# TensorE runs matmuls of no use during loads, at the head of each stage and in the first five items of each attention

## The chip, the cores and the metric

The kernel runs on one core of a Trainium2 chip. The core has five engines with a program each: TensorE (PE; its weight loads are listed as PEld), VectorE (DVE), ScalarE (ACT), GpSimd (POOL) and SyncE (SP, which issues DMAs). They meet through semaphores. The metric is the device time of one execution in microseconds (us). TensorE has two clock levels, 1.2 and 2.4 GHz; the profile shows the granted clock as a share of full speed.

## The reference

A residual stream x of 32 items of 128 rows by 128 columns passes through four layers of an attention-like block and a feed-forward-like block, each behind a layer norm:

```
x = x + _L0_xattn_ref(ctx, _layernorm(x), b, seq_len)      # 16 heads of 8, bias and length mask
x = x + _L0_ffn_ref(_layernorm(x), w1, w2)                 # summed experts
x = x + _L1_xattn_ref(_layernorm(x), ctx, lens, ...)       # depool
x = x + _L1_ffn_ref(_layernorm(x), mask, pos, router_w, ...)  # route 512 rows, attention, expand
x = x + _L2_xattn_ref(ctx, _layernorm(x), mask, b)         # 8 heads of 16
x = x + _L2_ffn_ref(_layernorm(x), w1, conv_w, conv_b, w2) # ternary weights, conv
x = x + _L3_xattn_ref(ctx, _layernorm(x), mask, ...)       # cross attention, 8 heads
x = x + _L3_ffn_ref(_layernorm(x), ...)                    # latent attention, 16 heads, causal; 4 experts
```

All of it is float32 in the reference, and the kernel returns the whole x.

## The kernel before, in words

Python code writes out the program of each engine, and each engine runs its program strictly in order; no scheduler moves anything. The work is cut into 15 stages, the list `phases`: prep (loads and constants), L0 attention, ffn0, depool, route, gather, L1 attention (four tiles, 16 heads), expand, L2 attention (8 heads), bit, cross, L3 attention (8 heads), latent, L4 attention (16 heads, causal), expert. At the end of each stage `phase_end` (L1022) drains an engine, raises `phase_done` and waits until all five have raised it. So no engine starts a stage before the slowest has ended the last one; what an engine waits for there is put down to L1022 in the profile.

Inside a stage, `steps` or `whole_steps` writes a software pipeline over the 32 items: in one step an engine works on several items at different lags. In an attention, PE's part is `attention_tensor`. At lag 1, `turns` transposes an item's queries and keys (L859, L860) and the split maxima of an item (L826). At lag 2, `halves` makes the raw scores: for each of four groups of heads it waits for a free PSUM bank (`raw_free`, which waits for `max_taken`, DVE's maximum over an earlier group), adds the bias (L746, `sel_bias`) and multiplies queries by keys (L753). DVE takes each row's maximum from that (L392, L397, L384). Later in the pipeline the scores are made again with the maximum taken off (L721 and L763, which multiplies by `sel_max`), ACT takes the exponential (L616, L620, L610), and PE multiplies by the values (L912). In L1 and L4 the first raw group comes with masks (`mask_strips`, `mask_whole`; the transposes of L799).

In ffn0, bit and cross the first PE work of an item is a transpose (L1041, L1033) of rows that ACT or DVE has normed; in route PE works twice for a short time (L1304, L1306); in latent PE first centres weights, then makes queries, then waits on `la_raw` and turns latents (L1799) into rows (L1806). `ident`, `identb` (bf16), `ones` and `sel_max` (bf16, 128 x 4 x 128) are constants that prep loads or makes.

PE had no work in prep. Before the change the only PE instructions are those that make results.

Of the kernel before, what the change touches and what calls it, by code (L numbers as in the profile page):

```python
# [135 lines left out]
def build(nc, t_in, out):  # L136
    with ExitStack() as ctx_:
# [26 lines left out]
        ones = sb("ones", [128, 128])  # L164
# [497 lines left out]
        def attention_tensor(pe, L, count, heads, mask_parts, mask, post_w):  # L662
# [34 lines left out]
            def halves(r_item, s_item, u):  # L697


                v = 1 - u  # L700
                whole = BANKS[L] == "items"
                r_groups = () if r_item is None else (u, 2 + u) if whole else (2 * u, 2 * u + 1)
                s_groups = () if s_item is None else (v, 2 + v) if whole else (2 * v, 2 * v + 1)
                if s_item is not None:
                    b, k = s_item
                    if u == (1 if whole else 0):
                        done(pe, "nmT_ready", b, count)
                    masked_scores = mask_parts and not cut_later
                    if whole and u == 0:
                        pe.wait_ge(*after("scores", b * 2 + 1))  # L710
                    for g in s_groups:
                        if whole and g == 0:
                            done(pe, "max_taken", b + 1, count)
                        elif not whole:
                            final_free(b, g)
                        bank, at = final_at(L, b, g, N)
                        for part in range(mask_parts if masked_scores else 0):
                            nc.tensor.matmul(ps[:, bank, at:at + N], mask(k, part), identb[:].unsqueeze(1).broadcast_to(four),
                                             start=part == 0, stop=False, skip_group_check=True)
                        if not masked_scores:  # L720
                            nc.tensor.matmul(ps[:, bank, at:at + N], kT[rows_of(g), k, :], qTm[rows_of(g), k, 0:N],  # L721
                                             start=True, stop=False, skip_group_check=True)
                    for g in s_groups if masked_scores else ():
                        bank, at = final_at(L, b, g, N)
                        nc.tensor.matmul(ps[:, bank, at:at + N], kT[rows_of(g), k, :], qTm[rows_of(g), k, 0:N],
                                         start=False, stop=False, skip_group_check=True)
                if r_item is not None:
                    b, k = r_item
                    if u == 0:
                        done(pe, "q_masked", b, count)  # L730
                        done(pe, "kT_ready", b, count)
                        if L in BIASES:
                            if b < 2:
                                pe.wait_ge(*after("early_nmT", b + 1))
                            else:
                                done(pe, "nmT_ready", b - 2, count)
                        if whole and b >= 4:
                            pe.wait_ge(*after("probs_ready", b - 3))
                    elif whole:
                        pe.wait_ge(*after("raw_scores", b * 2 + 1))  # L740
                    for g in () if whole else r_groups:
                        raw_free(b, g)
                    if L in BIASES:
                        for g in r_groups:
                            bank, at = raw_at(L, b, g, N)
                            nc.tensor.matmul(ps[:, bank, at:at + N], sel_bias[rows_of(g), :],  # L746
                                             nmT[rows_of(g), (k + 2) % RING, :].unsqueeze(1).broadcast_to([32, per, 128]),
                                             start=True, stop=False, skip_group_check=True)
                    for i in range(per):
                        for g in r_groups:  # L750
                            bank, at = raw_at(L, b, g, N)
                            dst = ps[:, bank, at + 128 * i:at + 128 * i + 128]
                            last = nc.tensor.matmul(dst, qTm[rows_of(g), k, 128 * i:128 * i + 128], kT[rows_of(g), k, :],  # L753
                                                    start=False, stop=True, skip_group_check=True)
                            if i == per - 1 and (raw_jobs(L) == 4 or g == r_groups[1]):
                                last.then_inc(sem("raw_scores"), 1)
                if s_item is not None:
                    b, k = s_item
                    for i in range(per):
                        for g in s_groups:  # L760
                            bank, at = final_at(L, b, g, N)
                            dst = ps[:, bank, at + 128 * i:at + 128 * i + 128]
                            last = nc.tensor.matmul(dst, sel_max[rows_of(g), i, :], nmT[rows_of(g), k, :], start=False,  # L763
                                                    stop=True, skip_group_check=True)
                            if i == per - 1 and (final_jobs(L) == 4 or g == s_groups[1]):
                                last.then_inc(sem("scores"), 1)
# [9 lines left out]
            def mask_strips(b, k):  # L776

                for a in range(2):
                    raw_free(b, a)
                if cut_later:  # L780
                    mask_tiles(b, (0, 1))
                    return
# [7 lines left out]
            def mask_whole(b, k):  # L790

                for a in range(2):
                    raw_free(b, 2 + a)
                if cut_later:
                    mask_tiles(b, (2, 3))
                    return
                for a in range(2):
                    for part in range(mask_parts):
                        nc.tensor.matmul(ps[:, raw_bank(L, b, 2 + a), 0:N], identb[:], mask(k, part).unsqueeze(1).broadcast_to(four),  # L799
                                         start=part == 0, stop=False, skip_group_check=True)  # L800
# [117 lines left out]
            def step(items):  # L918
# [12 lines left out]
                    mask_strips(*items[1])  # L931
                if L == "L0" and min(items) >= 3:
                    sum_products(pe, min(items) - 3)
            whole_steps(pe, count, TURN_LAG[post], step)


# [78 lines left out]

        phase_no = {}

        def phase_end(engine):

            n = phase_no.get(engine, 0) + 1  # L1020
# [68 lines left out]
            steps(act, B, [(1, take_rows(act))])  # L1089

        def ffn0_tensor(pe):
            def multiply(b, k):
                pe.wait_ge(*after("rowT", b + 1))
                wait_reuse(pe, after("added"), b, RING)
# [94 lines left out]
            steps(pool, B, [(3, take_patch)])  # L1189

        def depool_tensor(pe):
            def ends(b, k):
                pe.wait_ge(sem("dp_lens"), b + 1)
                wait_reuse(pe, after("dp_bound"), b, 2)
# [105 lines left out]
            nc.scalar.activation(small[:, 64:96], small[:, 0:32], ACT.Sin).then_inc(sem("ga_sines"), 1)  # L1300

        def route_tensor(pe):
            pe.wait_ge(sem("rt_wcol"), 1)
            nc.tensor.matmul(ps[0:B, 4, 0:128], wcol[:], ident[:], start=True, stop=True).then_inc(sem("rt_wT"), 1)  # L1304
            pe.wait_ge(sem("rt_coded"), 1)
            nc.tensor.matmul(ps[:, 5, 0:B], route_row[:, 384:512], ident[0:B, 0:B], start=True, stop=True)  # L1306
            nc.tensor.matmul(ps[:, 5, B:2 * B], route_row[:, 512:640], ident[0:B, 0:B], start=True,
# [6 lines left out]
        qD, kvD = q_all, kv_all  # L1314

        def gather_tensor(pe):
            pe.wait_ge(sem("ga_pick"), 1)


# [119 lines left out]
        pairT = probs[:, 1, 0:1024].rearrange("p (o t) -> p o t", o=2)  # L1439

        def expand_tensor(pe):


            for o in range(2):
                for T in range(TILES):
# [124 lines left out]
            steps(act, B, [(1, take_rows(act, dst=lambda k: xqT[:, k % 2, 1:129])), (2, silu)])  # L1570

        def bit_tensor(pe):
            def hidden(b, k):
                pe.wait_ge(*after("rowT", b + 1))
                wait_reuse(pe, after("bt_silu"), b, 2)
# [55 lines left out]
            steps(act, B, [(1, take_rows(act)), (2, take_kv), (3, take_q)])  # L1631

        def cross_tensor(pe):
            def queries(b, k):
                pe.wait_ge(*after("rowT", b + 1))
                wait_reuse(pe, after("cr_q"), b, 2)
# [141 lines left out]
            steps(act, PAIRS, [(0, scale), (1, take_turned), (3, take_v)])  # L1778

        def latent_tensor(pe):  # L1780
            pe.wait_ge(sem("la_weights"), 2)
            pe.wait_ge(sem("wo_loaded"), 16)
            nc.tensor.matmul(ps[:, 6, 384:384 + N_EXP3], wo_rows, w_h1[:, 320:], start=True, stop=True)
            nc.tensor.matmul(ps[:, 6, 0:320 + N_EXP3], centre[:], w_h1[:], start=True, stop=True).then_inc(sem("la_centred"), 1)

            def queries(b, k):
                pe.wait_ge(*after("rowT", b + 1))
# [4 lines left out]
                                 stop=True).then_inc(sem("used"), 1)  # L1792
            steps(pe, B, [(1, turn_x(pe)), (2, queries)])
            pe.wait_ge(sem("la_raw"), B)

            def turn_latents(p, k):
                pe.wait_ge(sem("la_latent"), 2 * p + 2)
# [280 lines left out]
                store(j)  # L2078

        def expert_tensor(pe):  # L2080
            def turn_block(j):
                pe.wait_ge(sem("bk_rows_%d" % (j % QUEUED)), 16 * (j // QUEUED + 1))
                if j >= 2:
# [294 lines left out]
        def row_counts(**more):  # L2378
# [2 lines left out]


        phases = [
            dict(sync=prep_sync, scalar=prep_scalar, gpsimd=prep_gpsimd, vector=prep_vector),
            dict(vector=lambda e: attention_vector(e, "L0", B, 16, True, False),
                 counts=attention_counts("L0", B, 16, False),
                 gpsimd=lambda e: attention_gpsimd(e, "L0", B, 16, True),
# [173 lines left out]
```

## Time and profile before

| | before |
|---|---|
| median of 3 runs | 1280.93 us |
| the three runs | 1286.64, 1275.42, 1280.93 us |
| profiled execution | 1290.61 us, its span 1288.9 us |
| mean granted TensorE clock in it | 0.894 |
| busy, share of the span | PE 86%, DVE 66%, PEld 63%, ACT 46%, POOL 28% |

The stages of the profiled execution begin at about these us of the span: prep 0, L0 17, ffn0 203, depool 226, route 290, gather 312, L1 334, expand 392, L2 420, bit 541, cross 684, L3 773, latent 900, L4 960, expert 1177. PE is the busiest engine in most of them; in depool it is DVE. The busy share is a mean over stages with different limits, so a stage is read by itself.

### The profile page before, as it was taken

What the parts mean: (1) busy time and instruction counts of PE and PEld (TensorE: products, weight loads), DVE (VectorE), ACT (ScalarE), POOL (GpSimd) and SP (SyncE); (2) the same over time, 40 slices, a digit from 0 to 9 for tenths busy, and PEclk for the clock granted to TensorE, in tenths of its full rate; (3) what the DMA queues carried; (4) which work ended last, traced back from release to release, by engine and by line L of the source; (5) the groups of instructions that cost most, each with busy time, mean ns of one, the idle gap of its engine ahead of it and who ended that gap; (6) DMA issues with size and microseconds to landing.
All of it is one profiled execution on the core that took longest, in us unless ns stands there. A gap on an engine that the chain in (4) does not pass through costs nothing. (4 is left out here: it accounts for less than half of the span.)

```text
span 1288.9 us, 36948 instructions
## 1 busy us (share of the span) xinstructions
PE 1110.1 (86%) x13741; PEld 811.3 (63%) x13741; DVE 845.1 (66%) x2666; ACT 591.9 (46%) x1413; POOL 357.2 (28%) x899
## 2 busy tenths in 40 slices
PE   2999998892894899689997999997899999896497
PEld 2888887672453677534444557885547887775497
DVE  4677766997636588679993226886845778953333
ACT  2688864565122466512222343554763445542243
POOL 1122220122040133400000001221433665573654
PEclk9999998795797599889996897998876999986899
DMA  9600000000000000110000005000000000024373
GB/s 288 186 8 3 4 3 2 2 2 1 1 2 1 2 3 3 65 68 1 1 1 0 1 1 194 3 3 2 1 1 2 3 4 3 11 74 117 129 235 109
DMA packets 36412, 49.43 MB, mean 38 GB/s; under 512 B 8365, under 2 KB 26161, under 8 KB 35904
## 3 DMA queue, kind: packets, MB, share of 16 engines
q1 hardware_dynamic: 32480, 40.55, 10.4%
q0 software_dynamic: 2752, 6.36, 1.4%
q8 instruction: 115, 1.88, 0.6%
q14 instruction: 57, 0.47, 0.1%
q10 hardware_dynamic: 1008, 0.16, 0.1%
HBM read 40.71 MB, written 11.81 MB: 41 GB/s over the span
## 5 line engine op out<-in xcount | busy, mean ns | idle before, releaser
L721 PE MATMUL ps<-qTm,kT 32*128 32x512 f32 (+1 forms) x1024 | 253.9, 560 | 3.7 <-ACT probs L620 3.4
L753 PE MATMUL ps<-kT,qTm 32*128 32x128 f32 x3200 | 254.9, 295 | 0.8 <-DVE kT L425 0.8
L753 PEld LDWEIGHTS ps<-kT,qTm 32*128 32x128 f32 x3200 | 230.5, 206 | 6.1 <-issue 3.4
L524 POOL CAST nm<-neg_max 128x16 bf16<-128x16 f32 (+1 forms) x132 | 26.9, 204 | 412.1 <-DVE neg_max L384 159.4
L620 ACT ACTIVATE probs<-ps 128x1024 f32<-128x1024 f32 x72 | 73.7, 1024 | 117.1 <-PE ps L763 116.6
L912 PE MATMUL ps<-probs,v_wide 128*32 128x128 f32 x3200 | 118.7, 283 | 9.1 <-DVE ctx_all L455 4.5
L397 DVE TENSOR_REDUCE neg_max<-ps 128x8 f32<-128x1024 f32 x72 | 87.9, 1221 | 57.3 <-PE ps L753 56.2
L721 PEld LDWEIGHTS ps<-qTm,kT 32*128 32x128 f32 x1024 | 86.2, 191 | 50.8 <-issue 39.8
L392 DVE TENSOR_REDUCE neg_max<-ps 128x4 f32<-128x512 f32 x128 | 82.2, 684 | 35.7 <-PE ps L753 35.6
L616 ACT ACTIVATE probs<-ps,bias_col 128x512 f32<-128x512 f32 x128 | 80.9, 683 | 37.5 <-PE ps L763 37.5
L411 DVE TENSOR_TENSOR qTm<-ps,hmask 128x512 f32<-128x512 f32 (+1 forms) x132 | 73.3, 555 | 37.4 <-ACT nmT L598 21.0
L912 PEld LDWEIGHTS ps<-probs,v_wide 128*32 128x32 f32 x3200 | 82.0, 112 | 24.9 <-issue 10.9
L763 PE MATMUL ps<-nmT,sel_max 32*128 32x128 bf16 x1600 | 97.2, 221 | 0.0
L1579 PE MATMUL ps<-tap_w,xqT 128*128 128x512 f32 x192 | 92.9, 621 | 0.0
L514 POOL COPY nm<-bias 128x12 bf16<-128x12 bf16 x96 | 19.0, 202 | 264.5 <-ACTq L1022 223.9
L626 ACT ACTIVATE pv<-ps 128x256 f32<-128x256 f32 x132 | 50.6, 383 | 77.1 <-PE ps L912 77.1
L610 ACT ACTIVATE probs<-ps,bias_col 128x1024 f32<-128x1024 f32 x64 | 71.3, 1114 | 32.0 <-PE ps L763 32.0
L879 PE MATMUL ps<-pv_pick,pv 128*128 128x72 f32 (+1 forms) x528 | 82.2, 279 | 0.9 <-ACT pv L626 0.9
L384 DVE TENSOR_REDUCE neg_max<-ps 128x8 f32<-128x1024 f32 x64 | 77.7, 1215 | 2.0 <-PE ps L753 1.7
L763 PEld LDWEIGHTS ps<-nmT,sel_max 32*128 32x128 bf16 x1600 | 72.5, 96 | 8.2 <-issue 5.9
L442 DVE RECIPROCAL inv_den<-ps 128x16 f32<-128x16 f32 (+1 forms) x132 | 30.2, 229 | 70.9 <-PE ps L879 67.3
L879 PEld LDWEIGHTS ps<-pv_pick,pv 128*128 128x128 f32 x528 | 70.5, 194 | 8.9 <-issue 1.8
(425 smaller groups left out, 2540.5 us busy)
## 6 DMA issues: line engine op xcount, KB each, us to landing
ctx_all<-in_W1T SPq DMA_DIRECT2D x38, 256.0 KB, 2.9
sorted_rows<-in_c_no_rows SPq DMA_DIRECT2D x1, 4940.0 KB, 20.8
kv_all<-sorted_rows SPq DMA_DIRECT2D x38, 130.0 KB, 2.6
ctx_all<-in_ctx SPq DMA_DIRECT2D x4, 1024.0 KB, 10.4
ctx_all<-in_ctxT SPq DMA_DIRECT2D x2, 2048.0 KB, 10.1
x_all<-in_x SPq DMA_DIRECT2D x4, 512.0 KB, 7.0
tap_w<-in_conv_wT SPq DMA_DIRECT2D x1, 768.0 KB, 6.6
out<-q_all,kv_all POOLq DMA_INDIRECT x38, 3.3
```

The costliest lines, as they stand in the source:

```text
L384: nc.vector.tensor_reduce(neg_max[:, k, 0:heads].rearrange("p (a h) -> p a h", a=2), ps[:, pair:pair + 2, 0:2 * N].rearrange("p a (h k) -> ...
L392: nc.vector.tensor_reduce(neg_max[:, k, per * g:per * g + per], ps[:, raw_bank(L, b, g), 0:N].rearrange("p (h k) -> p h k", h=per), AX.X, ...
L397: nc.vector.tensor_reduce(neg_max[:, k, H2 * u:H2 * u + H2].rearrange("p (a h) -> p a h", a=2), ps[:, 4 * u:4 * u + 2, 0:N].rearrange("p a ...
L411: nc.vector.tensor_tensor(qTm[:, k, 0:N].rearrange("p (i q) -> p i q", i=per), ps[:, 6, 0:128].unsqueeze(1).broadcast_to([128, per, 128]), ...
L616: nc.scalar.activation(probs[:, k % 2, N * g:N * (g + 1)], ps[:, final_bank(L, b, g), 0:N], ACT.Exp, bias=bias).then_inc(sem("probs_ready" ...
L620: nc.scalar.activation(probs[:, k % 2, 2 * N * u:2 * N * (u + 1)].rearrange("p (a n) -> p a n", a=2), ps[:, 2:4, 0:N], ACT.Exp, bias=bias) ...
L721: nc.tensor.matmul(ps[:, bank, at:at + N], kT[rows_of(g), k, :], qTm[rows_of(g), k, 0:N], start=True, stop=False, skip_group_check=True)
L753: last = nc.tensor.matmul(dst, qTm[rows_of(g), k, 128 * i:128 * i + 128], kT[rows_of(g), k, :], start=False, stop=True, skip_group_check=True)
L763: last = nc.tensor.matmul(dst, sel_max[rows_of(g), i, :], nmT[rows_of(g), k, :], start=False, stop=True, skip_group_check=True)
L879: last = nc.tensor.matmul(ps[:, 7, 256 + W * half:256 + W * half + W], pv[:, k % 2, 128 * half:128 * half + 128], pv_pick[:, 0 if heads == ...
L912: last = nc.tensor.matmul(ps[32 * j:32 * j + 32, 7, 128 * half:128 * half + 128], v_tile(k % 2, heads, 4 * half + j, i), probs[:, k % 2, 1 ...
L1579: last = nc.tensor.matmul(dst, xqT[:, k % 2, tap:tap + 128], tap_w[:, tap, :], start=False, stop=tap == 2)
```

## The change

`keep_busy(pe, spot, count)` writes `count` bf16 matmuls of 128 x 128 (`identb`) by up to 512 columns (`sel_max`) into a piece of PSUM, whose content nobody reads: the next real matmul there starts with `start=True`. `keep_busy_early` writes 44 float32 matmuls of 128 columns in prep, once `ones` is set. Heads: L0 16, ffn0 8, depool 14, route 64 and 11 more between its two PE groups, gather 9, L1 14, expand 8, L2 48, bit 46, cross 16, L3 8, latent 8 and then 12 and 20 inside, L4 8, expert 14; together 324 of 512 columns. In the first five items (`FILL`) of each attention, 4 x 512 columns per item are added right after the wait for the bank, ahead of the bias in L0, L2 and L3 (in L2 and L3 as pairs of 256 columns), and in `mask_strips` and `mask_whole` in L1 (all four items) and L4. Together these are 96 of 512 columns. No semaphore is new and no other engine's program changes; PE's later matmuls stay in their order. Behind the lines added, line numbers shift by up to 38 (L859 becomes L865, L746 becomes L748, L753 becomes L755).

PE at the head of L2, before: the last matmuls of expand (L1471), then the first item's transposes (L859, L860, L826), bias (L746) and raw scores (L753).

```order
L1471 MATMUL ps<-x_tiles,probs 128x128 x32
L859 MATMUL ps<-ident,row 128x128
L860 MATMUL ps<-ident,ctx_all 128x128
L826 MATMUL ps<-identb,nm 128x128
L746 MATMUL ps<-nmT,sel_bias 128x256 x2
L753 MATMUL ps<-kT,qTm 128x128 x4
```

PE at the head of L2 in the changed kernel (L1031 is the added matmul):

```order
L1500 MATMUL ps<-x_tiles,probs 128x128 x32
L1031 MATMUL ps<-sel_max,identb 128x512 x48
L865 MATMUL ps<-ident,row 128x128
L866 MATMUL ps<-ident,ctx_all 128x128
L832 MATMUL ps<-identb,nm 128x128
L1031 MATMUL ps<-sel_max,identb 128x256 x2
L748 MATMUL ps<-nmT,sel_bias 128x256
L1031 MATMUL ps<-sel_max,identb 128x256 x2
L748 MATMUL ps<-nmT,sel_bias 128x256
L755 MATMUL ps<-kT,qTm 128x128 x4
```

48 matmuls stand ahead of the first transpose, behind the stage's barrier, and two more ahead of each bias.

PE at the start of the program in the changed kernel, with what each row waits for: prep, then the head of L0 and its first items.

```order
L1038 MATMUL ps<-ones 128x128 [waits ones_set]
L1038 MATMUL ps<-ones 128x128 x43
L1031 MATMUL ps<-sel_max,identb 128x512 [waits phase_done]
L1031 MATMUL ps<-sel_max,identb 128x512 x15
L865 MATMUL ps<-ident,row 128x128 [waits q_row,ctx_loaded_0]
...
L1031 MATMUL ps<-sel_max,identb 128x512 [waits max_taken]
L748 MATMUL ps<-nmT,sel_bias 128x512
L1031 MATMUL ps<-sel_max,identb 128x512
L748 MATMUL ps<-nmT,sel_bias 128x512
L755 MATMUL ps<-kT,qTm 128x128 x8
```

The wait for the barrier now stands at the first matmul of the head, and the wait for DVE's maximum (`max_taken`) at the first added matmul of a group, no longer at the bias.

PE at the head of cross in the changed kernel, behind the last matmuls of bit (L1626):

```order
L1626 MATMUL ps<-w_q,qk_pad 128x128 x8
L1031 MATMUL ps<-sel_max,identb 128x512 x16
L1055 MATMUL ps<-ident,row 128x128
L1679 MATMUL ps<-bias_rows,onesb 128x256
L1681 MATMUL ps<-w_src,ctx_all 128x256 x2
```

16 stand ahead of the first item's transpose; the items themselves hold none.

```diff
--- before.py
+++ after.py
@@ -745,2 +745,4 @@
                             bank, at = raw_at(L, b, g, N)
+                            if b < FILL:
+                                keep_busy(pe, ps[:, bank, at:at + N], 512 // N)
                             nc.tensor.matmul(ps[:, bank, at:at + N], sel_bias[rows_of(g), :],
@@ -779,2 +781,4 @@
                     raw_free(b, a)
+                    if b < FILL:
+                        keep_busy(pe, ps[:, raw_bank(L, b, a), :])
                 if cut_later:
@@ -793,2 +797,4 @@
                     raw_free(b, 2 + a)
+                    if b < FILL:
+                        keep_busy(pe, ps[:, raw_bank(L, b, 2 + a), :])
                 if cut_later:
@@ -933,2 +939,3 @@
                     sum_products(pe, min(items) - 3)
+            keep_busy(pe, ps[:, 0, :], {"L0": 16, "L1": 14, "L2": 48, "L3": 8, "L4": 8}[L])
             whole_steps(pe, count, TURN_LAG[post], step)
@@ -1017,2 +1024,17 @@
 
+        FILL = 5
+
+        def keep_busy(pe, spot, count=1):
+
+            wide = spot.shape[1]
+            for _ in range(count):
+                nc.tensor.matmul(spot, identb[:], sel_max[:].rearrange("p i q -> p (i q)")[:, 0:wide], start=True, stop=True,
+                                 skip_group_check=True)
+
+        def keep_busy_early(pe):
+
+            pe.wait_ge(sem("ones_set"), 1)
+            for _ in range(44):
+                nc.tensor.matmul(ps[:, 0, 0:128], ones[:], ones[:], start=True, stop=True)
+
         def phase_end(engine):
@@ -1091,2 +1113,4 @@
         def ffn0_tensor(pe):
+            keep_busy(pe, ps[:, 7, :], 8)
+
             def multiply(b, k):
@@ -1191,2 +1215,4 @@
         def depool_tensor(pe):
+            keep_busy(pe, ps[:, 7, :], 14)
+
             def ends(b, k):
@@ -1302,4 +1328,6 @@
         def route_tensor(pe):
+            keep_busy(pe, ps[:, 7, :], 64)
             pe.wait_ge(sem("rt_wcol"), 1)
             nc.tensor.matmul(ps[0:B, 4, 0:128], wcol[:], ident[:], start=True, stop=True).then_inc(sem("rt_wT"), 1)
+            keep_busy(pe, ps[:, 7, :], 11)
             pe.wait_ge(sem("rt_coded"), 1)
@@ -1316,2 +1344,3 @@
         def gather_tensor(pe):
+            keep_busy(pe, ps[:, 7, :], 9)
             pe.wait_ge(sem("ga_pick"), 1)
@@ -1441,3 +1470,3 @@
         def expand_tensor(pe):
-
+            keep_busy(pe, ps[:, 7, :], 8)
 
@@ -1572,2 +1601,4 @@
         def bit_tensor(pe):
+            keep_busy(pe, ps[:, 7, :], 46)
+
             def hidden(b, k):
@@ -1633,2 +1664,4 @@
         def cross_tensor(pe):
+            keep_busy(pe, ps[:, 7, :], 16)
+
             def queries(b, k):
@@ -1780,2 +1813,3 @@
         def latent_tensor(pe):
+            keep_busy(pe, ps[:, 7, :], 8)
             pe.wait_ge(sem("la_weights"), 2)
@@ -1784,2 +1818,3 @@
             nc.tensor.matmul(ps[:, 6, 0:320 + N_EXP3], centre[:], w_h1[:], start=True, stop=True).then_inc(sem("la_centred"), 1)
+            keep_busy(pe, ps[:, 7, :], 12)
 
@@ -1794,2 +1829,3 @@
             pe.wait_ge(sem("la_raw"), B)
+            keep_busy(pe, ps[:, 7, :], 20)
 
@@ -2080,2 +2116,4 @@
         def expert_tensor(pe):
+            keep_busy(pe, ps[:, 7, :], 14)
+
             def turn_block(j):
@@ -2383,3 +2421,3 @@
         phases = [
-            dict(sync=prep_sync, scalar=prep_scalar, gpsimd=prep_gpsimd, vector=prep_vector),
+            dict(sync=prep_sync, scalar=prep_scalar, gpsimd=prep_gpsimd, vector=prep_vector, tensor=keep_busy_early),
             dict(vector=lambda e: attention_vector(e, "L0", B, 16, True, False),
```

## Rows read from the trace of the kernel before

**Rows 1.** Table by stretch: length, busy PE, PEld, DVE, ACT, POOL (us), clock, DMA, GB/s.

```profile
205.00:213.00 8.00, 6.83 (x30) 5.78 (x30) 4.38 (x17) 3.67 (x14) 0.78 (x2) 0.57 0.01 3
226.00:240.00 14.00, 9.14 (x35) 7.13 (x35) 11.52 (x65) 5.70 (x20) 1.19 (x3) 0.52 0.00 1
291.00:318.00 27.00, 5.68 (x126) 5.15 (x130) 19.91 (x112) 14.16 (x35) 6.87 (x21) 0.51 0.00 1
334.00:342.00 8.00, 8.00 (x50) 3.74 (x49) 4.25 (x11) 0.72 (x2) 0.00 (x0) 0.50 0.01 2
390.00:400.00 10.00, 6.25 (x17) 3.96 (x18) 4.58 (x20) 3.75 (x7) 1.34 (x3) 0.52 0.00 0
414.00:445.00 31.00, 20.49 (x194) 15.02 (x194) 18.03 (x55) 8.74 (x20) 3.31 (x18) 0.50 0.00 1
541.00:557.00 16.00, 4.77 (x7) 1.98 (x8) 11.80 (x30) 2.47 (x6) 7.07 (x8) 0.50 0.67 264
558.00:570.00 12.00, 11.83 (x47) 5.17 (x45) 9.73 (x41) 3.11 (x7) 0.00 (x0) 1.00 0.00 0
690.00:717.00 27.00, 27.00 (x61) 14.37 (x61) 3.61 (x13) 5.92 (x20) 0.00 (x0) 0.50 0.00 1
933.00:946.00 13.00, 11.98 (x31) 4.32 (x31) 3.75 (x6) 10.21 (x30) 3.56 (x5) 0.50 0.00 0
960.00:987.00 27.00, 25.54 (x265) 18.93 (x267) 13.56 (x18) 4.87 (x9) 4.99 (x11) 0.51 0.00 1
1177.00:1185.00 8.00, 5.48 (x22) 4.62 (x23) 1.97 (x12) 2.44 (x9) 0.00 (x0) 0.50 0.29 86
```

**Rows 2.** PE's timeline, L1: start, duration, operation, idle time before and its releaser.

```profile
339.52 2.77 PE L799 MATMUL ps<-kv_all,identb 128*128 128x512 bf16 x6
...
346.29 1.46 PE L799 MATMUL ps<-kv_all,identb 128*128 128x512 bf16 x6
```

**Rows 3.** PE's timeline, L0: turns of items and one raw group.

```profile
20.84 0.45 PE L859 MATMUL ps<-ident,row 128*128 128x128 f32 x1 [20.84 <-ACT row L584]
...
29.33 0.61 PE L746 MATMUL ps<-nmT,sel_bias 32*128 32x512 bf16 x2 [0.88 <-DVE neg_max L392]
...
55.97 0.27 PE L859 MATMUL ps<-ident,row 128*128 128x128 f32 x1
...
103.81 0.27 PE L859 MATMUL ps<-ident,row 128*128 128x128 f32 x1
```

**Rows 4.** PE's timeline, the opening of L1.

```profile
333.73 0.48 PE L859 MATMUL ps<-ident,kv_all 128*128 128x128 f32 x1 [3.60 <-SPq L1022]
```

**Rows 5.** ACT's (first row) and PE's timeline, L2.

```profile
419.57 0.20 ACT L259 ACTIVATE table_junk<-ones 128x1 f32<-128x1 f32 x1 [14.74 <-SPq L1022]
...
423.03 0.47 PE L859 MATMUL ps<-ident,row 128*128 128x128 f32 x1 [11.20 <-ACT row L584]
...
449.31 0.28 PE L859 MATMUL ps<-ident,row 128*128 128x128 f32 x1
...
487.24 0.28 PE L859 MATMUL ps<-ident,row 128*128 128x128 f32 x1
```

**Rows 6.** PE's timeline, the opening of bit.

```profile
553.08 0.60 PE L1577 MATMUL ps<-bias_rows,onesb 3*128 3x512 bf16 x1
```

**Rows 7.** ACT's (first row) and PE's timeline, cross.

```profile
683.81 0.20 ACT L259 ACTIVATE table_junk<-ones 128x1 f32<-128x1 f32 x1 [3.34 <-POOLq L1022]
...
686.87 0.44 PE L1033 MATMUL ps<-ident,row 128*128 128x128 f32 x1 [3.85 <-DVE row L269]
...
717.53 0.42 PE L1033 MATMUL ps<-ident,row 128*128 128x128 f32 x1
...
722.17 0.27 PE L1033 MATMUL ps<-ident,row 128*128 128x128 f32 x1
```

**Rows 8.** PE's timeline, the second half of latent.

```profile
933.89 1.05 PE L1799 MATMUL ps<-ident,o_sb 128*128 128x128 f32 x2 [5.39 <-ACT o_sb L1764]
```

**Rows 9.** PE's timeline, the opening of L4.

```profile
959.73 0.30 PE L859 MATMUL ps<-ident,q_all 128*128 128x128 f32 x1 [1.82 <-POOLq L1022]
```


## What I expect

> **What bounds the kernel now.** I read the views in this order: the table of the granted TensorE clock by stretch, PE's timeline at the heads of the stages, then what the other engines do there. The result gives a mean granted clock of 0.894 for the profiled execution. The table [rows 1] shows that this is no even shade: a stretch stands at 0.50 to 0.57 or at 1.00, which are TensorE's levels of 1.2 and 2.4 GHz. A mean of 0.894 then means (1 - 0.894) x 2 = 21% of the span, 273 us, at the lower level. Nearly all of it lies at heads of stages. The price shows at one line [rows 2]: six bf16 transposes of 128x512 take 2.77 us at the lower level and 1.46 at the higher, 0.46 and 0.24 each. A useless matmul has that size, so those are its two prices (0.45 and 0.23 below, as the six include one pipeline's end).
>
> What the lower level costs is not 273 us. Only PE's own time is halved, and only where PE sets the pace. In expand and L2 [rows 1] PE is busy 6.25 of 10 and 20.49 of 31 us; in the depool row DVE is busy 11.52 of 14, PE 9.14. In the cross row PE is busy 27.00 of 27 us at 0.50. That is the dearest stretch.
>
> Every stage ends in a barrier of five engines, and PE's program is in order. A head of useless matmuls therefore starts when the barrier opens, never in the idle time before it, and real work waits until it is through. So each head is weighed: what fits between the barrier and PE's first real operand is free, the rest is delay.
>
> **What a head costs.** In bit, dense work starts at 553.08 [rows 6], the row to 557 reads 0.50 and the row from 558 reads 1.00 [rows 1]: the clock rose after some 4.5 us. Two other rows are slower: in L1 PE is busy 8.00 of 8 us at 0.50, in cross 27.00 of 27. I take 4.5 us, thus ten matmuls at 0.45 and the rest at 0.23: 8 cost 3.6, 14 cost 5.4, 16 cost 5.9, 46 cost 12.8, 48 cost 13.2 us. Lower bound: all at 0.23; upper bound: all at 0.45. The useless matmuls inside the first items come when the clock should be up: 4 x 512 columns in each of five items, 20 x 0.23 = 4.6 us per attention (16 in L1: 3.7).
>
> **Stage by stage, gains positive, in us.** In brackets the bounds.
>
> - **Early 44 in prep**: beside loads; nothing of PE runs before 20.84 [rows 3]. 0.
> - **L0**: the turns L859 start 20.84, ... 55.97: six steps in 35.13 us, later 4.78 each (55.97 to 103.81 are ten) [rows 3]. At that pace six are 28.7: 6.4 lost. The page grants the first 50 us a clock of 1.00, but L859 takes 0.45 there and 0.27 at 55.97: durations decide, it is the lower level. In an early item PE waits 0.88 for DVE's maximum [rows 3], and a useless matmul sits behind that wait, in the loop, so some of the gain goes. The head of 16 ends about 0.3 to 2.5 late. +4.5 (0 to +6).
> - **ffn0**: PE 6.83 busy at 0.57 [rows 1], half of that at most; its 8 end by the first operand if the clock is still up from L0. +2 (0 to +3).
> - **Depool**: DVE covers it [rows 1]; were that cover gone, half of PE's 9.14. 0 (-1 to +2).
> - **Route and gather**: PE 5.68 busy in 27 us, mostly waiting for DVE; the 64, 11 and 9 lie in the waits. +2 (0 to +2.8).
> - **L1**: PE's wait of 3.60 before 333.73 is released by the barrier (L1022) [rows 4]: real work is ready, so 5.4 of delay, and 3.7 inside, against half of 8.00. -4.5 (-9 to 0).
> - **Expand**: 3.6 of delay against half of 6.25 plus a little. 0 (-2 to +1).
> - **L2**: the stage opens at 419.57 by ACT's first row, PE's first operand comes at 423.03 [rows 5]; the 11.20 idle there lies mostly before the barrier. 48 end at 432.8: 9.7 late. The seven steps to 449.31 take 26.3 where the later pace ((487.24 - 449.31)/12 = 3.16) gives 22.1; at most 4.2 come back, less the fills inside. -6 (-10 to -3).
> - **Bit**: 46 end near 554.2, real work began at 553.08 [rows 6]; up to half of its 4 cold us comes back. 0 (-2 to +2).
> - **Cross**: stage opens 683.81, first operand 686.87, eight steps in 30.66 us to 717.53; the next two take 4.64 [rows 7], so eight at the higher level are 18.6. 12.1 come back; 16 end 2.8 late. +9.5 (-4 to +12).
> - **L3**: no row quoted; built like L2, with 8: late by 1.8 to 3.6, back 2 to 3. -1 (-4 to +1).
> - **Latent**: the first 8 are about 1 late; the last 20 (4.6 to 9) lie in the 5.39 that PE waits for ACT's o_sb [rows 8]; PE is then busy 11.98 of 13 at 0.50, at most 6 back; ACT is busy 10.21 there and sets the next limit. +4.5 (-2 to +5).
> - **L4**: PE starts right at the barrier [rows 9]: 8 are 1.8 to 3.6 late; PE 25.54 busy of 27 at 0.51 [rows 1], 12.8 back, less most of 4.6 inside. +7 (0 to +10).
> - **Expert**: 14 ahead of ready work, 5.4, against half of 5.48 and a little behind it. -1.5 (-4 to +1).
>
> Sum: +16.5. On the profiled execution (1290.61 us, span 1288.9) that gives 1274.1; that run lies 9.7 above the median of the three shown. If the excess is a longer stay at the lower level in cross, whose 30 us are unlike any other stage, the change removes the excess too and 1274 holds; if it lies elsewhere, 1280.93 - 16.5 = 1264.4. I take **1268**, between the two.
>
> **Rivals.**
>
> *The heads run at the higher level from their start.* PE was at work shortly before most barriers, and at L4's opening L859 takes 0.30, nearly the 0.27 of the higher level [rows 3, 9]. Then ten matmuls cost 2.2 us less in each of L1, L2, bit, cross, L3, L4 and expert: 15 us less, about 1253 (1246 to 1260). Against it: 11.20 us idle before L2. Chance 0.24.
>
> *The lower level costs little, the useless work takes it back.* Where PE waits for DVE or ACT, a faster PE waits longer. With cross at 9.5, but 1 each for L0, ffn0 and gather, 2 for latent, 3 for L4, and -6, -8, -2, -3 for L1, L2, L3, expert, the sum is -1.5: about 1282 on the median, 1276 to 1293. For it: 20.49 of 31 in L2. Against it: 25.54 of 27 in L4. Chance 0.24. The Trainium skill, "TensorE: Matmul & The Clock Gate", Part 1 (The HAM clock gate), speaks for this one: it says "For modeling, the ramp penalty is <1% of a typical kernel span"; by that rule at most some 13 us could come back and the heads' delay would eat them. The trace disagrees with the premise, for 21% of this span is at the lower level, not one ramp.
>
> *Useless work does not lift the clock: slower.* In cross PE was busy for all of 27 us and the level stayed at 0.50. If the heads meet the same, each of the 420 (324 at heads, 96 inside items, counted in 512 columns) costs 0.45 and nothing comes back: L2 is 18 late, bit 9, L1 and expert 6 each, L0, L3, L4 and latent 4 to 13 each with what lies inside; 80 us in all if half the inside is hidden, 1300 for a third of the stages and 1370 for all. It decides from about 150 matmuls at 0.45 (150 x 0.22 = 33 us lost against the sum). Against it: the level did rise under bf16 transposes in L1 [rows 2] and under bit's matmuls. Chance 0.07.
>
> The forecast itself, 1260 to 1276, has 0.45.
>
> **Numbers.** About 1% tells this kernel from no change: below 1268 is faster, above 1294 slower. Faster: 0.23 of the second case and not quite half of the forecast, 0.43. Slower: 0.07, and 0.02 for the upper bounds of delay: 0.09. The rest, 0.48, is the same. The range 1250 to 1288 takes in the forecast, most of the heads-at-once case and most of the little-back case; some 0.07 lie below it, 0.12 above.
>
> **What would show it.** The granted clock should read 1.00 from about 5 us after each head; the mean should go from 0.894 to 0.95 or so. Cross: steps of 2.3 us from the first. L4: 0.27 for L859 from its first item. L2's first real matmul should come near 433, 13 us behind its barrier instead of 3.5; if it comes at 430, the heads ran at the higher level. L1 and L2 should each be longer than before by some 5 us. I am wrong if cross still has a long stretch at 0.50, if L1 and L2 don't lengthen, or if the gain comes from stages I put at 0.

## The result, and the profile after

The changed kernel takes 1309.91 us (median of 4 runs, 1307.55 to 1313.95) against 1278.18 us (4 runs): ratio 1.0245, 95% interval 1.0199 to 1.0291. It is slower by 2.5%; I had forecast 1268, with a range from 1250 to 1288. Its profiled execution took 1307.55 us, span 1305.7, with a mean granted clock of 0.946 where before had 0.894. So the change did what it says to the clock, and the time went the other way.

The page's lines for busy time and granted clock of the changed kernel:

```profile
PE 1184.8 (91%) x14262; PEld 831.9 (64%) x14289; DVE 845.5 (65%) x2666; ACT 590.4 (45%) x1413; POOL 357.2 (27%) x899
PEclk9599999899898799999999999999899999997899
```

One slice stands out: the second reads 5. It is L0. Cut at the barriers (the last drain of each stage), the stages last, in us. The columns "before, 3rd" and "before, 4th" are the third and fourth profiled executions of the kernel before, told below; at 1279.86 us the fourth is the one nearest the median.

| stage | before, 1st | before, 3rd | before, 4th | changed | heads only | no L0 items | items only | trimmed |
|---|---|---|---|---|---|---|---|---|
| L0 | 186.1 | 185.3 | 186.7 | 206.2 | 183.1 | 182.3 | 215.2 | 186.9 |
| L1 | 58.4 | 58.3 | 58.4 | 64.3 | 60.2 | 62.4 | 60.2 | 55.7 |
| L2 | 121.9 | 120.3 | 120.4 | 132.8 | 127.3 | 133.8 | 142.6 | 120.6 |
| bit | 142.4 | 143.4 | 143.4 | 140.9 | 140.8 | 141.3 | 142.7 | 140.9 |
| cross | 89.0 | 77.0 | 77.0 | 77.0 | 78.2 | 76.9 | 80.0 | 76.9 |
| L3 | 127.0 | 128.0 | 129.7 | 132.9 | 126.7 | 132.8 | 150.2 | 128.8 |
| latent | 59.9 | 55.9 | 59.6 | 56.4 | 56.8 | 56.4 | 59.7 | 56.7 |
| L4 | 217.5 | 210.5 | 214.4 | 210.4 | 213.9 | 213.0 | 214.2 | 210.8 |
| expert | 111.3 | 112.7 | 113.2 | 113.9 | 113.9 | 114.4 | 113.3 | 113.0 |
| the other six | 175.1 | 174.5 | 174.9 | 170.4 | 169.4 | 170.6 | 174.7 | 171.8 |
| all | 1288.3 | 1265.9 | 1277.6 | 1305.2 | 1270.3 | 1284.0 | 1352.6 | 1262.0 |

From the fourth execution of before to the changed kernel: L0 +19.5, L2 +12.4, L1 +6.0, L3 +3.3, expert +0.7; L4 -4.1, latent -3.2, bit -2.4, the other six -4.5; cross 0. That is the loss: four attentions lose 41 us, and all that was won elsewhere is 14. Of these 14, the 7.3 of L4 and latent are no wider than the spread of the kernel before: its third execution has 210.5 and 55.9 there, as short as the changed kernel, with no useless matmul in it.

**L0.** In what follows a filler is one of the useless matmuls, and a pair is two groups of heads with their two biases. The table by stretch of the changed kernel (columns as in [rows 1]):

```profile
22.00:32.00 10.00, 7.26 (x58) 4.44 (x59) 3.87 (x6) 2.62 (x10) 0.56 (x3) 0.98 1.04 291
32.00:42.00 10.00, 10.00 (x50) 5.39 (x49) 3.27 (x5) 1.31 (x5) 0.79 (x4) 0.50 0.84 230
42.00:52.00 10.00, 9.53 (x60) 5.44 (x60) 3.27 (x5) 3.55 (x9) 0.38 (x3) 0.50 0.70 185
52.00:62.00 10.00, 9.53 (x41) 4.10 (x42) 1.98 (x3) 2.24 (x7) 0.42 (x3) 0.50 0.64 180
```

The head did lift the clock, and it fell again at 31.6 us, with PE 9.5 to 10 of 10 us busy for the next 30. PE's timeline there, one raw group of an early item at the higher level, one at the lower, and the turns of two items (L865 was L859):

```profile
24.56 0.39 PE L1031 MATMUL ps<-sel_max,identb 128*128 128x512 bf16 x1 [1.44 <-DVE qTm L411]
24.88 0.39 PE L748 MATMUL ps<-nmT,sel_bias 32*128 32x512 bf16 x1
25.20 0.39 PE L1031 MATMUL ps<-sel_max,identb 128*128 128x512 bf16 x1
25.52 0.38 PE L748 MATMUL ps<-nmT,sel_bias 32*128 32x512 bf16 x1
...
43.54 0.47 PE L865 MATMUL ps<-ident,row 128*128 128x128 f32 x1
...
53.26 0.61 PE L1031 MATMUL ps<-sel_max,identb 128*128 128x512 bf16 x1
53.80 0.60 PE L748 MATMUL ps<-nmT,sel_bias 32*128 32x512 bf16 x1
54.33 0.61 PE L1031 MATMUL ps<-sel_max,identb 128*128 128x512 bf16 x1
54.87 0.60 PE L748 MATMUL ps<-nmT,sel_bias 32*128 32x512 bf16 x1
54.87 1.67 PE L755 MATMUL ps<-kT,qTm 32*128 32x128 f32 x11
...
57.11 0.47 PE L865 MATMUL ps<-ident,row 128*128 128x128 f32 x1
```

Each of the four now starts 0.32 us after the last at the higher level and 0.54 at the lower. Before, the two biases of 32 rows stood side by side as one row of x2 ([rows 3]), and the first raw product (L753) followed 0.37 us behind their start at 29.33:

```profile
29.70 1.94 PE L753 MATMUL ps<-kT,qTm 32*128 32x128 f32 x16
```

So up to its first raw product a pair costs 1.61 us (53.26 to 54.87) where two biases alone took 0.37, and one step from turn to turn takes 13.6 us (43.54 to 57.11), against 6.3 to 6.7 in the kernel before at the same level.

Two pairs per step explain 2.5 of the 6.9 us between 13.6 and 6.7. Most of the rest stands at L721, the scores with the maximum taken off, which belong to another item. In the kernel before, three of the eight of a step start among the raw products; here is PE's timeline of its step from 37.89 to 44.59:

```profile
38.62 1.43 PE L721 MATMUL ps<-qTm,kT 32*128 32x512 f32 x2
38.94 0.61 PE L746 MATMUL ps<-nmT,sel_bias 32*128 32x512 bf16 x2
...
39.63 1.06 PE L721 MATMUL ps<-qTm,kT 32*128 32x512 f32 x1
39.75 0.44 PE L753 MATMUL ps<-kT,qTm 32*128 32x128 f32 x2
...
41.03 2.32 PE L721 MATMUL ps<-qTm,kT 32*128 32x512 f32 x3
42.35 0.61 PE L746 MATMUL ps<-nmT,sel_bias 32*128 32x512 bf16 x2
```

In the changed kernel's step from 43.54 they stand in two blocks between the pairs:

```profile
44.26 2.28 PE L721 MATMUL ps<-qTm,kT 32*128 32x512 f32 x4
...
49.95 1.06 PE L721 MATMUL ps<-qTm,kT 32*128 32x512 f32 x1
...
50.80 2.52 PE L721 MATMUL ps<-qTm,kT 32*128 32x512 f32 x3
```

They hold PE nearly by themselves for 2.3 and 3.3 us (49.95 to the filler at 53.26), where it was 0.3 and 1.3 before (38.62 to 38.94, 41.03 to 42.35): some 4 us more. A filler of 128 rows parts not only the two biases of its pair but also the work of other items that ran beside it.

**L2's and cross's heads.** PE's timeline of the changed kernel:

```profile
441.32 11.96 PE L1031 MATMUL ps<-sel_max,identb 128*128 128x512 bf16 x47 [7.66 <-SPq L1044]
453.12 0.27 PE L865 MATMUL ps<-ident,row 128*128 128x128 f32 x1
```

```profile
715.00 4.75 PE L1031 MATMUL ps<-sel_max,identb 128*128 128x512 bf16 x15 [1.22 <-POOLq L1044]
719.59 0.27 PE L1055 MATMUL ps<-ident,row 128*128 128x128 f32 x1
...
723.19 0.27 PE L1055 MATMUL ps<-ident,row 128*128 128x128 f32 x1
725.41 0.27 PE L1055 MATMUL ps<-ident,row 128*128 128x128 f32 x1
```

L2's first real matmul now stands 12.3 us behind the barrier (440.86) where it stood 3.5 behind [rows 5]. Cross runs in steps of 2.2 us from the start; in [rows 7] its first eight took 3.8 each.

The seven fillers that the trace shows at the head of L3 took 1.67 us (from 791.83), and so did seven at the head of L4 (from 981.20): 0.24 each, the higher level from the start.

### The profile page after: what moved, and what is told of

It reads as the page before. It is cut to its first block and busy times, and to the rows that moved or that the text cites. A ratio compares the mean times of both kernels' runs of the same rounds, so it can differ in the third digit from the quotient of the medians.

```text
span 1305.7 us, 38009 instructions
## 1 busy us (share of the span) xinstructions
PE 1184.8 (91%) x14262; PEld 831.9 (64%) x14289; DVE 845.5 (65%) x2666; ACT 590.4 (45%) x1413; POOL 357.2 (27%) x899
## 5 line engine op out<-in xcount | busy, mean ns | idle before, releaser
L721 PE MATMUL ps<-qTm,kT 32*128 32x512 f32 (+1 forms) x1024 | 245.8, 543 | 3.6 <-ACT probs L620 3.1
L755 PE MATMUL ps<-kT,qTm 32*128 32x128 f32 x3200 | 241.6, 281 | 0.4 <-DVE kT L425 0.4
L755 PEld LDWEIGHTS ps<-kT,qTm 32*128 32x128 f32 x3200 | 214.0, 192 | 3.7 <-issue 2.4
L1031 PE MATMUL ps<-sel_max,identb 128*128 128x512 bf16 (+1 forms) x433 | 116.0, 402 | 39.6 <-SPq L1044 21.9
L721 PEld LDWEIGHTS ps<-qTm,kT 32*128 32x128 f32 x1024 | 83.8, 185 | 48.8 <-issue 38.0
L1031 PEld LDWEIGHTS ps<-sel_max,identb 128*128 128x128 bf16 x460 | 43.3, 106 | 104.4 <-issue 33.6
L765 PE MATMUL ps<-nmT,sel_max 32*128 32x128 bf16 x1600 | 94.3, 217 | 0.0
L514 POOL COPY nm<-bias 128x12 bf16<-128x12 bf16 x96 | 18.9, 201 | 250.3 <-ACTq L1044 210.5
```

What stands on the lines that cost most here:

```text
L1031: nc.tensor.matmul(spot, identb[:], sel_max[:].rearrange("p i q -> p (i q)")[:, 0:wide], start=True, stop=True, skip_group_check=True)
```

## The experiments

Ratios are to the kernel before, run beside it on the same chip, with their 95% intervals.

**1. Heads only.**

```diff
-        FILL = 5
+        FILL = 0
```

> The heads stay, the 96 matmuls inside the first items go (FILL = 0). Theory A, the matmuls inside cost the time: a 128-row matmul between matmuls of 32 rows stops those from running side by side, 1.7 us each in L0 at the lower level. Then L0 falls from 206 us to about 186, L3 from 133 to 128, L2 from 133 to 128, L1 from 64 to 61, and the time is about 1265 (ratio 0.99). Theory B, the clock fell in L0 at 31 us by itself and the matmuls inside cost only 0.23 to 0.45 each: L0 stays above 198, the time about 1295.

Measured: 1272.67 us, ratio 0.996 (0.9925 to 0.9995). L0 183.1, L2 127.3, L3 126.7, L1 60.2, as theory A said, if 8 us above its total. The 96 matmuls inside the items are worth 1.0245 - 0.996 = 2.9%, 36 us. The clock falls in L0 here too, to a shorter stretch (31 to 45 us):

```profile
31.00:45.00 14.00, 14.00 (x136) 11.37 (x136) 7.04 (x12) 6.43 (x17) 1.58 (x8) 0.51 0.73 198
```

So part of theory B holds: the fall comes without the items. What it costs depends on what then stands in the loop.

In L2 and L3 the items did hold the level, and the stages were longer all the same. Without them the clock falls soon behind the head, here in L2 and L3 of this run:

```profile
430.00:441.00 11.00, 10.19 (x113) 7.43 (x113) 5.76 (x10) 3.36 (x8) 2.33 (x13) 0.53 0.01 2
765.00:775.00 10.00, 9.79 (x91) 7.07 (x89) 5.03 (x10) 1.84 (x4) 2.08 (x11) 0.50 1.05 385
```

In the changed kernel it doesn't, in L2 and in cross and L3:

```profile
445.00:575.00 130.00, 123.24 (x1973) 87.60 (x1973) 82.37 (x195) 67.36 (x131) 38.76 (x159) 1.00 0.02 4
718.00:919.00 201.00, 196.53 (x2322) 135.75 (x2321) 106.79 (x308) 87.92 (x197) 24.64 (x128) 1.00 0.10 33
```

Yet L2 takes 132.8 us with the items and 127.3 without, L3 132.9 and 126.7.

**2. Items only.** The edit takes out all `keep_busy` lines of the heads and the early ones; those under `if b < FILL` stay.

> The 96 matmuls inside the first items stay, all heads and the early ones in prep go. Theory A: L0 pays 20 us or more, L1, L2 and L3 4 us each, L4 about the same as before, cross as long as before (77 to 89 us): about 1310 (ratio 1.025). Theory B: they cost 0.23 to 0.45 each, about 30 us at most, less what a higher clock returns: 1280 to 1290.

Measured: 1353.2 us, ratio 1.0612 (1.0542 to 1.0682), far beyond both. Without heads the useless matmuls meet the lower level and hold up the steps there. The table by stretch of this run, L2 and L3 (PE, then clock):

```profile
451.00:500.00 49.00, 45.15 (x311) 25.69 (x311) 14.68 (x32) 11.07 (x24) 4.86 (x24) 0.50 0.00 1
817.00:861.00 44.00, 43.03 (x290) 24.36 (x291) 12.35 (x25) 5.66 (x11) 3.61 (x19) 0.51 0.40 140
```

L2 and L3 stay at the lower level for 50 and 44 us; in the kernel before it was 25 and 14. PE is busy for 45.15 of 49 us and the level does not rise: matmuls of this mix did not lift it, and the slow stretch is longer with them. Cross, with nothing added, took 80.0 us here, the first hint that its 89 was not fixed.

**3. The change without the items of L0.**

```diff
-                            if b < FILL:
+                            if b < FILL and L != "L0":
```

> The change without the 20 matmuls inside L0's first five items; everything else as changed. Theory A: L0 returns from 206 to about 186 us and the time from 1310 to about 1290 (ratio to before 1.01). Theory B: the clock falls in L0 all the same, L0 stays above 198 and the time above 1300.

Measured: 1287.13 us, ratio 1.0079 (1.0041 to 1.0117); L0 182.3. The 20 useless matmuls in L0 alone cost 1309.91 - 1287.13 = 23 us, 1.1 each, where I had 0.23.

**4 and 5. What makes them dear: rows or order.** Both keep the change, and put both useless matmuls of a pair ahead of both biases; the first also narrows them to the 32 rows of their group. This is the edit of the first, without the lines that give `keep_busy` its argument for the rows; the second is the same without `rows_of(g)`.

```diff
+                        for g in r_groups if b < FILL else ():
+                            bank, at = raw_at(L, b, g, N)
+                            keep_busy(pe, ps[:, bank, at:at + N], 512 // N, rows_of(g))
                         for g in r_groups:
                             bank, at = raw_at(L, b, g, N)
-                            if b < FILL:
-                                keep_busy(pe, ps[:, bank, at:at + N], 512 // N)
```

> The change, but the matmuls inside the items of L0, L2 and L3 take 32 rows, those of the group they stand in, and stand ahead of both biases of a pair, so that two groups can run side by side; as many columns as before. Theory A (the 128-row matmul stops matmuls of 32 rows from running side by side): the first six steps of L3 go from 25.5 to about 21 us, L2's from 28.4 for seven to 25, L0 from 206 to 185-192; the time about 1285 (ratio 1.005). Rival (each matmul costs its columns, whatever its rows): steps as in the change, 1310. If the clock falls with fewer rows, L3's opening shows a stretch at 0.50 and the steps lie between.

> The change with only the order of the narrow_items run: inside L0, L2 and L3 both useless matmuls of a pair stand ahead of both biases, but they keep 128 rows. Theory A (the rows matter, not the order): the two biases run side by side again, the useless ones do not, so part of the price stays: L0 near 200, first six steps of L3 near 24, time about 1303 (ratio 1.02). Rival (the order made the difference in narrow_items): L0 near 188, L3's six steps near 21.7, time about 1287 (ratio 1.005).

Measured: 32 rows 1286.56 us, ratio 1.0038 (1.0014 to 1.0063), as theory A said. 128 rows in the new order 1291.92, ratio 1.0138 (1.0072 to 1.0203; three of four runs 1289 to 1292, one 1307 at a mean clock of 0.936 against 0.949 to 0.956), between the two expectations; L0 189.1, as the rival said, and L3's six steps 23.0 (changed 25.4, 32 rows 21.7, heads only 19.1). My theory A, rows alone, falls: order and rows both count. The first pair of L3, at the higher level, shows the shares. Heads only, then 32 rows, then 128 rows in the new order, then the change:

```profile
762.40 0.28 PE L748 MATMUL ps<-nmT,sel_bias 32*128 32x256 bf16 x2 [1.17 <-DVE kT L425]
762.51 0.62 PE L755 MATMUL ps<-kT,qTm 32*128 32x128 f32 x8
```

```profile
771.54 0.40 PE L1032 MATMUL ps<-sel_max,identb 32*128 32x256 bf16 x4 [1.17 <-DVE kT L425]
771.75 0.29 PE L749 MATMUL ps<-nmT,sel_bias 32*128 32x256 bf16 x2
771.86 0.63 PE L756 MATMUL ps<-kT,qTm 32*128 32x128 f32 x8
```

```profile
775.69 0.60 PE L1032 MATMUL ps<-sel_max,identb 128*128 128x256 bf16 x4 [1.17 <-DVE kT L425]
776.22 0.28 PE L749 MATMUL ps<-nmT,sel_bias 32*128 32x256 bf16 x2
776.34 0.61 PE L756 MATMUL ps<-kT,qTm 32*128 32x128 f32 x8
```

```profile
794.95 0.38 PE L1031 MATMUL ps<-sel_max,identb 128*128 128x256 bf16 x2 [1.17 <-DVE kT L425]
795.26 0.28 PE L748 MATMUL ps<-nmT,sel_bias 32*128 32x256 bf16 x1
795.47 0.39 PE L1031 MATMUL ps<-sel_max,identb 128*128 128x256 bf16 x2
795.80 0.28 PE L748 MATMUL ps<-nmT,sel_bias 32*128 32x256 bf16 x1
795.80 0.72 PE L755 MATMUL ps<-kT,qTm 32*128 32x128 f32 x8
```

From the pair's first row to its first real product (L755, L756) it takes 0.11, 0.32, 0.65 and 0.85 us. Two biases side by side cost 0.11. Useless matmuls of 32 rows add 0.21, those of 128 rows 0.54, and pulling the two biases apart 0.20 more: 0.74 per pair. Ten pairs are 7.4; L3's six steps lost 25.4 - 19.1 = 6.3. In L0 the run with the 128 rows in the new order kept the higher level after its first 3 us (L866 there takes 0.27 to 0.33 us), so that L0 shows what order and level do together: six steps take 36.3 us there and 53.4 in the change; without the items (experiment 3) it is 28.4. What the level alone did to L0 was not tried apart from the order.

**6 and 7. The head of cross alone, 16 and 4.** On the kernel before:

```diff
         def cross_tensor(pe):
+            keep_busy(pe, ps[:, 7, :], 16)    # or 4
```

> The kernel before with the 16 matmuls at the head of cross alone. Theory A (the head lifts the clock and the stage keeps it): cross goes from 89 to 77-78 us, the time from 1278 to 1267 (ratio 0.991), no other stage moves. Rival (how long cross stays at the lower level is set elsewhere, as the 80 us without a head in the run with the matmuls inside the items alone suggest): cross between 80 and 89, ratio 0.995 to 1.

> The kernel before with 4 matmuls at the head of cross instead of 16; they take 1.8 us at the lower level and end before the first operand, 3 us behind the barrier. If any useless work there lifts the clock, cross takes 77 us and loses no 2 us of delay; if the stretch of matmuls has to go on into the real work, cross stays near 89, ratio 1.0.

Measured: 16 gives 1275.39, ratio 0.9953 (0.9922 to 0.9985); 4 gives 1280.76, ratio 1.0012 (0.9991 to 1.0033). Both profiles have cross at 77 us (77.5 and 77.0), yet 16 win 0.5% (0.2 to 0.8), some 6 us, and 4 win nothing. A stage that is 12 us shorter in the profile and a time that moves by half of that or not at all: then the comparison with the first profile is at fault. The 16 end late, with the first real matmul 5.5 us behind the barrier; with 4 it stands 3.0 behind, and the level stays low for 7.5 us.

**8 to 10. The kernel before, three more times.**

> The kernel before once more, for a second profile. The runs of before lie 1275 to 1287 us; the first profiled execution was 1290.6. If the excess lies in cross, whose 30 us at the lower level were the longest of any stage, cross is about 10 us shorter here than its 89 us and the time near 1278; if not, another stage is.

> The kernel before a third time. Both profiled executions so far had cross at 89 us and lay 8 to 12 us above the median of the timed runs. If the long stay at the lower level in cross comes in some executions only, one near 1278 shows cross at 77 to 80 us; if it comes in all, cross is 89 again and the time 1286 to 1291.

> The kernel before a fourth time, with the same question as before_3: cross at 77 to 80 us in an execution near 1278, or 89 again near 1288.

Measured: 1286.54, 1268.22 and 1279.86 us, with cross at 89.0, 77.0 and 77.0. The table by stretch of cross in the second and the fourth execution of the same kernel:

```profile
686.00:713.00 27.00, 27.00 (x62) 13.98 (x60) 3.72 (x13) 6.05 (x20) 0.00 (x0) 0.50 0.00 1
```

```profile
684.00:691.00 7.00, 4.28 (x11) 2.64 (x12) 2.97 (x14) 1.15 (x4) 0.00 (x0) 0.50 0.00 0
692.00:719.00 27.00, 27.00 (x111) 15.73 (x110) 6.56 (x24) 10.79 (x36) 0.00 (x0) 1.00 0.00 1
```

The same program stays at the lower level for 34 us or for 7, doing 62 or 111 instructions in 27 us. The first two executions, 8 to 12 us above the median, had the long stay. The timed runs leave no record by stage, so how many of them have the long one is open: of the 19 runs of the kernel before that stand beside experiments 1 to 3, eight took 1281 to 1284 us at a mean clock of 0.899 to 0.901, much like the second execution (0.900, long), and eleven took 1267 to 1279 at 0.904 to 0.914, like the fourth (0.903) and third (0.915), both short. Cross isn't all that moves: over the four executions L4 lasts 217.5, 215.1, 210.5 and 214.4 us, latent 59.9, 59.9, 55.9 and 59.6.

**11 and 12. What remains worth having.** "Trimmed" keeps the items in L4 alone, drops the heads of L1, L3, L4 and expert, and cuts L2's to 14; one of the lines changed:

```diff
-            keep_busy(pe, ps[:, 0, :], {"L0": 16, "L1": 14, "L2": 48, "L3": 8, "L4": 8}[L])
+            keep_busy(pe, ps[:, 0, :], {"L0": 16, "L1": 0, "L2": 14, "L3": 0, "L4": 0}[L])
```

> From the change only what paid in the stages measured so far: matmuls inside the items in L4 alone; heads as in the change in prep, L0, ffn0, depool, route, gather, expand, bit, cross and latent; none in L1, L3, L4 and expert; 14 instead of 48 in L2, which end by the first operand 3.5 us behind the barrier. Theory A (delay of heads with ready work, and price inside the items): against before L0 -2, ffn0 -1.5, gather and route -2.5, expand -1, L2 -1, bit -1.4, cross -11, latent -3, L4 -3, together -26: about 1252 (ratio 0.98), with L1, L3 and expert as before. Theory C (a head pays by what the stages behind it keep of the clock, so L1 and L3 without one lose as much as they save): no better than the kernel with all heads, 1270.

Measured: 1268.98 us, ratio 0.9899 (0.9864 to 0.9934): faster than both kernels by the times, though half of what I expected; 11 of the 26 us expected were cross's, which is at 77 us in the third and fourth executions of before as well. The time is the one that theory C named, but not by its way: L1 without a head takes 55.7 us, less than with one or in the kernel before, and its first real matmuls meet 2.9 us of the lower level where the kernel before has 8.9. L2 takes 120.6 us, as before (120.3 to 122.0): its 14 end 5.5 us behind the barrier, not 3.5. "Shorter" cuts L0 and L2 to 8 and cross to 8.

> The trimmed kernel with shorter heads where they still ended behind the first operand: L0 8, L2 8, cross 8. If delay is what they cost and 8 are enough to lift the clock: L0 and L2 2 us shorter each, cross 77 as with 4 and with 16, time about 1264 (ratio 0.987). If 8 are too few, L2's opening shows the lower level to 25 us as in the kernel before, and nothing is won: 1270.

Measured: 1264.56, ratio 0.9892 (0.9854 to 0.9929), no different from trimmed. L2's opening stayed at 0.50 for 25 us (121.9 us in all), so 8 were too few there, while cross took 75.4. L0 stayed at the lower level for 33 us behind its barrier and took 186.8 us, no longer than with 16 (186.9).

## Why the prediction was wrong, point by point

**The step that failed** is the price inside the items: "20 x 0.23 = 4.6 us per attention", because they "come when the clock should be up". It has two faults. The price was read from a dense run of equal matmuls [rows 2] and applied to single ones among matmuls of 32 rows that ran side by side; there a pair cost 0.74 us at the higher level, not 0.46 (experiments 4 and 5). And in L0 the clock was not up: it fell behind the head, and the same 20 cost 23 us (experiment 3). In L2 and L3 they cost 5.5 and 6.2 us (changed against heads only), in L1 4.1, close to my 3.7. The clock alone doesn't explain L0: my price for the lower level was 0.45, or 9 us for 20, and they cost 1.1 each. What the sum had at nothing is the work that no longer runs side by side: the two biases of a pair, and L721 of another item. Only in L4 did they no harm: its first six steps take 28.1 us in five profiles with them (changed, no L0 items, both of experiments 4 and 5, trimmed) and 30.5 with the heads only, though the whole stage shows no clear gain (210.4 to 214.7 against 213.9). There both fillers stand ahead of a pair's masks, and L721 still runs beside the raw products:

```profile
992.68 0.70 PE L721 MATMUL ps<-qTm,kT 32*128 32x512 f32 x2
992.69 0.71 PE L755 MATMUL ps<-kT,qTm 32*128 32x128 f32 x8
```

The level holds at 1.00 there, where it falls to 0.50 for 13.7 us with the heads only (from 952.6). That this place is why was not tried by itself.

**The second error is the base.** +9.5 for cross was right for the profiled execution (12.0 us came back) and too much for the median, where 16 at the head of cross alone gave some 6 us. I had named it ("the change removes the excess too and 1274 holds"), but put 1268 between the two readings. With cross at 0 to 6 the sum against the median is +7 to +13, not +16.5; that alone still leaves a gain. Nor was cross's stay "unlike any other stage": [rows 1] has L2 at 0.50 for 31 us and L4 at 0.51 for 27.

**What held.** The clock rises some 3 to 6 us into a head: behind the barrier the lower level lasted 3.8 us in L2, 3.2 in cross and 5.9 in L1. Heads ahead of ready work are delay: L1's first real matmul stands 5.9 behind the barrier (I had 5.4), L2's is 8.8 later than before (9.7). ffn0, gather and route gave 4.8 together against 4 forecast. For latent (3.2 against 4.5) and L4 (4.1 against 7) it can't be said: set against each of the four executions of before, latent comes out between -0.5 and 3.5, L4 between 0.1 and 7.1. L3 was forecast at -1; its head was about even (126.7 us without the items; 127.0 to 129.6 before) and the items took the 6. The signs that I had named came true, the mean clock (0.946), cross's steps, L4's 0.27 and L2's 12.3 us, but for the 1.00 behind each head, which L0 broke at 31.6. Nearly all of them look at the heads; none looks at the length of a step that holds fillers, where the time was lost.

**The rivals.** *The heads run at the higher level from their start* held in L3 and L4 (0.24 each) and not in L1, L2, bit, cross and expert. The slower one had the right sign and the wrong mechanism: it priced heads that don't lift the clock, and those of L1, L2 and cross did. In one place its premise was right, inside L0, L2 and L3 of the run with items only, where PE was busy and the level stayed. The rival in which useless work takes back what the clock gives had the right shape, but it put 1276 to 1293: its losses were in L1, L2, L3 and expert, and it kept a gain of 1 for L0, where 19.5 us were lost.

The sentence of the Trainium skill ("TensorE: Matmul & The Clock Gate", Part 1), that the ramp penalty is under 1% of a span, was set aside because 21% of this span is at the lower level. Measured, the best version recovered 1.1% (0.7 to 1.5), its heads' delay taken off; its profiled execution still has a mean clock of 0.927. So the share of the span was the wrong measure for what these heads can win. What all of the lower level costs no run here shows, so the sentence is neither borne out nor refuted.

## What to carry to other kernels

A filler matmul costs what it does to its neighbours, so price it from the rows it will stand between, at both clock levels. Here 128-row fillers between 32-row matmuls that run side by side cost far more than their columns, and 32-row ones less. A head of fillers has to be long enough to lift the clock and short enough to end by the first real operand; in L2 none of the three lengths did both (8 did not lift it, 14 and 48 ended late). Before a gain is counted from a slow stretch of a profile, see whether a second execution has that stretch.

## What the runs showed that was not expected

- The same program stayed at the lower level in cross for 34 us in two executions and for 7 in two, with PE busy for 27.00 of 27 us of the long stay. What sets it is open.
- In L0 the clock fell about 14 us behind the barrier in the changed kernel and with the heads only, and not in the run with the 128 rows in the new order. PE had waited 1.44 us ahead of the first raw group in the change and in that run alike; why the level fell was not tried. With L0's program the same, heads and no items, it stayed low for 13.7, 6.8 and 17.1 us (heads only, no L0 items, trimmed) and L0 took 183.1, 182.3 and 186.9.
- The trace of the kernel before holds no record of the clock ahead of 49 us, and that of the items only none ahead of 83.6, and the views print 1.00 there. The durations are those of the lower level (a turn of 128x128 takes 0.42 to 0.47 us up to 75.2 with the items only, 0.27 from 85.3), so the mean clocks of these runs are too high by that much.
